# Attention plus expert layer on one core: ones laid by transfers, tables loaded ahead, multiplies before the first chunk, one chunk's remainder moved

## The reference

```
x = x + layernorm(attention(layernorm(x)))        # 16 heads, causal softmax, output projection, biases
x = x + layernorm(experts(layernorm(x)))          # top 2 of 8 experts per sequence, exact gelu, mean of both
# layernorm(x) = (x - mean) / sqrt(var + 1e-5), over the 256 features
```

## Time and profile before

| | us |
|---|---|
| median of three runs (lowest, highest) | 2064.71 (2061.21, 2065.99) |
| the profiled execution | 2067.85 |
| its span, first to last instruction | 2066.1 |
| PE, DVE, ACT, POOL busy in the span | 1978.9, 1799.9, 1362.3, 316.4 |
| mean granted TensorE clock | 0.985 |

### The profile page before, as it was taken

The page is one execution under the profiler, slowest core; times in us unless marked ns, Lnnn a source line. Parts: engine busy times, 40 slices in busy tenths (PEclk is TensorE's granted clock), DMA queues, the critical chain, the costliest instruction groups (busy, mean ns, idle before and its releaser), DMA issues.

```text
span 2066.1 us, 39584 instructions
## 1 busy us (share of the span) xinstructions
PE 1978.9 (96%) x15700; PEld 863.7 (42%) x15700; DVE 1799.9 (87%) x3564; ACT 1362.3 (66%) x1651; POOL 316.4 (15%) x366
## 2 busy tenths in 40 slices
PE   6999999999999999999999999999999996999997
PEld 3655333333333333333333333333333324666664
DVE  6876799999999999999999999999899917899873
ACT  3766657777777777777777777777777781333332
POOL 5333201010110101011100101011010104322000
PEclk9999989999999999999999999999999998999998
DMA  4877613150504224030513314050422034453220
GB/s 124 254 242 207 156 26 67 28 90 8 89 18 85 47 48 82 16 89 13 85 32 68 71 26 89 7 90 20 82 48 50 17 104 108 123 148 108 82 67 31
DMA packets 144651, 162.40 MB, mean 79 GB/s; under 512 B 52690, under 2 KB 118354, under 8 KB 144466
## 3 DMA queue, kind: packets, MB, share of 16 engines
q1 hardware_dynamic: 137554, 147.26, 30.5%
q0 software_dynamic: 6912, 12.61, 2.7%
HBM read 99.77 MB, written 59.77 MB: 77 GB/s over the span
## 4 chain that ended last, share of the span: by engine, by line
PE 79%; DVE 13%; ACT 4%; issue 1%; SPq 1%; DMA 1%; POOL 0%; ACTq 0%; DVEq 0%; POOLq 0%
PE b_psO L1103 25%; PE b_psS L1086 25%; PE b_ring L605 13%; PE a_psQK L888 6%; DVE b_pmax L621 3%; PE a_psV L900 3%; PE c_psH L1483 3%; PE c_psO L1496 2%; ACT b_prob L1050 2%; PE b_ring L603 1%; DVE c_attn L105 1%; DVE c_ln_f_stats L81 1%; DVE c_ln_x_stats L81 1%; PE c_psA L1453 1%; DVE c_x L1314 1%
## 5 line engine op out<-in xcount | busy, mean ns | idle before, releaser
L621 DVE TENSOR_REDUCE b_pmax<-b_ring 128x1 f32<-128x512 f32 (+4 forms) x2284 | 1336.6, 647 | 82.1 <-PE b_ring L605 65.1
L1050 ACT ACTIVATE b_prob<-b_psS 128x1024 f32<-128x1024 f32 (+3 forms) x1280 | 1085.1, 895 | 372.2 <-PE b_psS L1086 367.5
L1086 PE MATMUL b_psS<-g_qT,g_kT 64*128 64x512 bf16 (+6 forms) x5120 | 837.5, 349 | 10.0 <-ACT b_prob L1050 7.2
L605 PE MATMUL b_ring<-g_kT,g_qT 64*128 64x512 bf16 (+2 forms) x2500 | 717.5, 349 | 4.0 <-DVE b_pmax L621 2.6
L1103 PE MATMUL b_psO<-b_prob,g_v 128*32 128x512 f32 (+3 forms) x5120 | 597.3, 542 | 0.3
L1086 PEld LDWEIGHTS b_psS<-g_qT,g_kT 64*128 64x128 bf16 (+1 forms) x5120 | 296.6, 94 | 462.9 <-ACT b_prob L1050 343.4
L1021 POOL TENSOR_SCALAR_AFFINE_SELECT b_prob<-b_prob 128x512 f32<-128x512 f32 x256 | 164.5, 643 | 1321.1 <-ACT b_prob L1050 1320.9
L605 PEld LDWEIGHTS b_ring<-g_kT,g_qT 64*128 64x128 bf16 x2500 | 221.7, 94 | 236.3 <-DVE b_pmax L621 163.7
L603 PE MATMUL b_ring<-later,query_of 64*128 64x128 bf16 x988 | 192.4, 220 | 1.9 <-DVE b_pmax L621 1.3
L1103 PEld LDWEIGHTS b_psO<-b_prob,g_v 128*32 128x32 f32 x5120 | 103.6, 108 | 174.2 <-issue 132.8
L1483 PE MATMUL c_psH<-c_yT,c_w1e 128*128 128x512 f32 x256 | 121.0, 618 | 20.8 <-ACT c_hT L1408 20.7
(11 more groups left out here) (113 smaller groups left out, 1059.4 us busy)
## 6 DMA issues: line engine op xcount, KB each, us to landing
qk_parts<-a_parts SPq DMA_DIRECT2D x64, 384.0 KB, 4.6
g_qT<-qk_parts SPq DMA_DIRECT2D x184, 128.0 KB, 3.9
g_kT<-qk_parts SPq DMA_DIRECT2D x184, 128.0 KB, 5.2
out_sums<-b_outT SPq DMA_DIRECT2D x64, 256.0 KB, 2.6
v_ones<-a_v SPq DMA_DIRECT2D x16, 544.0 KB, 6.0
g_v<-v_ones SPq DMA_DIRECT2D x32, 272.0 KB, 5.3
a_x<-in_L_attn_x SPq DMA_DIRECT2D x16, 512.0 KB, 4.8
c_x<-in_L_attn_x SPq DMA_DIRECT2D x16, 512.0 KB, 6.9
```

Source lines behind the costliest of these rows:

```text
L605: ins_ = self.nc.tensor.matmul(to, groups.qT[own, g, h // 2, 0, t * P:(t + 1) * P], groups.kT[own, g, h // 2, 0, pc * CH:pc * CH + w], sta ...
L621: self.nc.vector.tensor_reduce(pmax[:, c % 2].rearrange("p (h t) n -> p h t n", t=TT)[:, heads[0]:heads[-1] + 1:2, qt, pc], bank[:, 0:k * ...
L1050: nc.scalar.activation(prob[:, j % PBUF, 2 * s:2 * s + 2, off:CH], psS[:, 2 * s:2 * s + 2, off:CH], ACT.Exp).then_inc(exp_done, 1)
L1086: ins_ = nc.tensor.matmul(psS[:, 2 * s + p, off:CH], kT[own, g, s, ab, kt * P:(kt + 1) * P], qT[own, g, s, ab, c * CH + off:(c + 1) * CH], ...
```

## The change

`write_ones` now fills a small tile of ones, 128 partitions of 16 elements, and clears the part of `g_v`. A new method `lay_ones` starts eight DMAs on POOL's queue, after the tables of `build_rest`; each copies the small tile into one row of 2048 elements of the key tile, and stage B's PE waits for them. ACT takes a root of a constant as its first instruction, and an exponential of it during chunk 14, both into a tile `a_ready` that nobody reads. PE multiplies the identity with itself 36 times into the value bank before it waits for the first chunk, and waits for the weights after the first transposes instead of before them. The last chunk's middle part, low part and store move from key steps 1, 3 and 6 to 26, 30 and 34.

```diff
-    SET_ONES = 3
+    SET_ONES = 2
+    LAID = 2 * 2 * HP
...
+        self.ones_laid = ctx.enter_context(nc.semaphore("g_ones_laid"))
+        self.ones = ctx.enter_context(nc.sbuf_tensor("g_ones", [P, S // P], BF16))
...
     def write_ones(self, pool):
+        self.nc.gpsimd.memset(self.ones[:, :], 1.0).then_inc(self.ones_set, 1)
+        self.nc.gpsimd.memset(self.vS[:, :, :, HG * VC:VROW].rearrange("p g t n -> p (g t) n"), 0.0
+                              ).then_inc(self.ones_set, 1)
+
+    def lay_ones(self, eng):
+        eng.wait_ge(self.ones_set, self.SET_ONES)
         for p in range(2):
             row = p * HALF + KB
-            self.nc.gpsimd.memset(self.kT[row:row + 1, :, :, 1, :], 1.0).then_inc(self.ones_set, 1)
-        pool.wait_ge(self.ones_set, 2)
-        self.nc.gpsimd.memset(self.vS[:, :, :, HG * VC:VROW].rearrange("p g t n -> p (g t) n"), 0.0
-                              ).then_inc(self.ones_set, 1)
+            for g in range(2):
+                for s in range(HP):
+                    eng.dma_start(self.kT[row:row + 1, g, s, 1, :].rearrange("o (p n) -> o p n", p=P),
+                                  self.ones[:, :]).then_inc(self.ones_laid, 16)
...
-REST_MIDDLE_AT = 1
-REST_LOW_AT = 3
-REST_STORED_AT = 6
+REST_MIDDLE_AT = 26
+REST_LOW_AT = 30
+REST_STORED_AT = 34
...
+        WARM = 36
...
+        ready = sb("a_ready", [P, 2], F32)
...
             consts.build_rest(pool)
+            groups.lay_ones(pool)
...
             act.wait_ge(consts.set, consts.EPS_SET)
+            nc.scalar.activation(ready[:, 0:1], consts.eps[:, :], ACT.Sqrt)
             root(0)
...
                 if n + 2 < N:
                     root(n + 2)
+                elif n + 2 == N:
+                    nc.scalar.activation(ready[:, 1:2], consts.eps[:, :], ACT.Exp)
...
             pe.wait_ge(consts.set, consts.IDENT)
+            for i in range(WARM):
+                nc.tensor.matmul(psV[:, i % TT, 0:P], ident[:, :], ident[:, :], start=True, stop=True)
+            turn(0)
             pe.wait_ge(w_ld, 5 * 16)
-            turn(0)
...
-            pe.wait_ge(groups.ones_set, Groups.SET_ONES)
+            pe.wait_ge(groups.ones_laid, 16 * Groups.LAID)
```

## The result

| | before | changed |
|---|---|---|
| median of 11 runs each (us) | 2065.99 | 2052.11 |
| lowest, highest | 2058.71, 2071.63 | 2046.39, 2056.98 |
| profiled execution, its span | 2067.85, 2066.1 | 2049.51, 2047.8 |

The ratio is 0.9937, 95% interval 0.992 to 0.9953: 13.9 us less by the medians, where 12.8 were forecast. The measured median is within 0.2 us of the forecast of 2052.

The account below looks back on a forecast made before the run. PE (96% busy) was taken to bound the kernel, with DVE (87%) where it is later. Start 10.0 plus stage B 5.5 minus new places 2.7 gave 12.8 us off 2064.71, so 2052 us, range 2049 to 2056 (8 in 10: 2046 to 2059).

Parts of the forecast that it names:

- Memsets and first table load: Start of stage A: without the memsets' delay of DVE (6.7 us) and the table load (1.28), first chunk 8.0 us earlier.
- PE's own multiplies are late next: Start of stage A: multiplies end at 11.9 us, then transposes and copy, first L888 at 13.8, a gain of 7.1 us.
- Full clock for chunk 0: Chunk 0's first query-key matmuls take 6.87 us instead of 9.75 if the clock is up: 2.9 us gained.
- What hides: POOL's eight issues end at 13 to 14.5 us with 10 us of cover; chunk 14's early exponential costs 0, at most 0.2.
- third rival: Laying the ones is slow, 2.5 us per issue, so POOL is free at 28 us: 2055 to 2056 us; chance 0.06.
- Stage B's first 30 us: 217.77 to 247.8 us: table load, low and middle part go; gain 5.5 us, between 3.5 and 7.5.
- none there: Near 231 us in stage B: no clock dip expected once the wait for the low part and the table load are gone.
- The new places: Stage B: low part at step 30 costs 2.2 us, middle part at step 26 0.5, stores 0; together -2.7 us.
- second rival: The dip at 286 us, 13.6 us at half clock, goes too as PE's rhythm changes: 2048 us; chance 0.17.
- A low part with a dip behind it: First rival: the low part at step 30 stops PE and the clock falls, up to 5.1 us more: 2057; chance 0.17.
- A clock that is not held: Fourth rival: the multiplies do not raise the clock, L888 starts at 19.9 us, the start gives 1.0: 2061; chance 0.10.
- Two dips in the first group: Fifth rival: the clock falls repeatedly from 218 us; two more dips eat the gain, three or more give 2071; chance 0.06.

Follow-up runs that it names:

- e1: Kernel before with only the ones laid by eight transfers instead of two memsets: chunk 1's matmuls start 6.7 us earlier; 73.5 us to step 22.
- e12: The changed kernel itself, timed again on one chip with the POOL version: median 2051.75 us, ratio 0.9934 to the kernel before.
- e3: Changed kernel without the 36 multiplies: first query-key matmul at 13.23 us, chunk 1 at 26.25 against 24.96.
- e4: Changed kernel with the last chunk's middle part, low part and store back at steps 1, 3 and 6: 73.0 us to step 22 instead of 66.1.
- e2: Kernel before with only the 36 multiplies and the moved wait for the weights: first query-key matmul at 21.03 us, chunk 1 0.4 us later.
- e6: Kernel before with the two memsets cut in four each: L888 started at 20.39 us instead of 20.94; 73.5 us to step 22.
- e7: Changed kernel with only the middle part back at step 1: 66.8 us to step 22, 115.3 to step 38.
- e10: Changed kernel with the last chunk's middle and low part on POOL and 28 multiplies instead of 36: chunk 1 at 26.40 us, ratio 0.9918 to the kernel before.
- e5: Changed kernel without the early exponential in chunk 14: 67.6 us to step 22, 1.5 us later; 120.2 to step 38.

## Why the prediction was right, step by step

- **Memsets and first table load.** 8.0 us forecast; the first chunk was ready at 9.4 us, as said, from a start of the statistics 0.2 us later. e1 shows the memsets' share, 6.7 us at chunk 1.
- **PE's own multiplies are late next.** Forecast start of L888 13.8, measured 13.70, on the path that was forecast: the chain goes through L896, then the transposes, then the copy. But three terms were off and cancelled. The clock rose 3.6 us after the first multiply and not 5.3 (the first 17 records stand in 3.6 us, 0.21 each; 5 or 6 weight loads per us up to 4.6 us, 10 or 11 from 5.3 on); by the prediction's own prices the block would have ended at 11.1, and it ended at 11.63, about half of that because a record took 0.112 us at full clock and not 0.107; and transposes, copy and hand-overs took 2.07 instead of 1.87. The moment of the rise varies from run to run: 3.0 to 5.7 us after the first multiply in the eight traces, 3.6 in the changed kernel and 4.9 in e12, which is the same kernel. What sets it is not shown.
- **Full clock for chunk 0.** 2.9 us forecast, 9.89 - 7.24 = 2.65 measured. But e3 shows that leaving the multiplies out costs only 1.3 us: the slow records there took 8.85 us, not 9.75, and L906 started 0.5 us earlier. The larger part of stage A's gain, 8.6 of 9.9 us in these two traces, needs no multiplies.
- **What hides.** POOL was free at 12.2 us (eight issues, 4.69 us), before the 13 to 14.5 forecast, and 12 us ahead of L787 at 24.61. Three of the eight issues ran beside the four L105 and took 0.64 to 0.77 us; the five behind them took 0.54 each (lines in the last section). So POOL's issues were at most 0.23 us longer beside instructions of 0.41 us, and the four L105 took 1.38. The third rival's 2.5 us for one issue did not come; the dearest of the eight took 0.77. The exponential ahead of time cost stage A nothing: 9.89 us of gain at chunk 1 and 9.88 at the last chunk.
- **Stage B's first 30 us: the term that was mis-sized.** 5.5 us forecast. Against the one trace it was 8.0, like with like 73.5 - 66.1 = 7.4. What failed is "DVE cannot be fed without a gap through a ring of three banks": it is, for 21.02 us. The floor that I had worked out, 22.5 us, was the answer, and I took the middle between two bounds instead of asking which engine was left to stop DVE. The reason given for the dip at 231 us, the wait for the low part, fits the profile of before and e4; in e1, e2 and e6 the clock fell ahead of the low part, behind the table load. The prediction removed both, so its "none there" came true.
- **The new places.** -2.7 forecast, -3.8 measured. Low: 2.2 forecast, 2.1 measured. Middle: 0.5 forecast, 1.7 measured; I read ACT's busy share (18.68 of 25) as slack, but an exponential behind the 1.89 us is what PE waits for next, and PE waited 1.8 us. At step 1 the same part costs 0.7.
- **The sum.** Stage B 5.5 - 2.7 = 2.8 forecast, 3.5 measured like with like; stage A 10.0 forecast, 8.9 to 10.2 measured in eight traces against the one profile of before. Together 12.4 to 13.7, and 13.9 by the medians. Two errors of about 1 us and 2 us in stage B had opposite signs, and so had those of the first start; that the median was met to 0.1 us is partly luck.
- **The rivals.** The dip at 286 is neither fixed nor caused by the change: it was 13.7, 6.8 or 0 us in the traces, with and without the change. So the second rival can't be told from scatter. A low part with a dip behind it came in e7. A clock that is not held came in e10. Two dips in the first group came in the changed stage B in e5 and e7, three in no trace.

Not settled: what decides the length of the second dip, and whether the clock falls behind the table load. The second dip's place is after the stretch with DVE full, in every kernel that shows it. Of the 11 timed runs of the changed kernel the three fastest (2046.4 to 2049.5 us) have a mean clock of 0.990 to 0.992 and the four slowest (2056.0 to 2057.0) one of 0.986 to 0.988, so much of the scatter goes with time at half clock. In the traces most of that time lies in stage C (35.5 us in the changed kernel's trace, against 6.8 in the first group), which I didn't study.

## What to carry to other kernels

Look at what a long instruction on few partitions keeps from running elsewhere: 13.9 us of memsets on one partition, on an idle engine, cost 6.7 us at the start, and cutting them did not help. When the first waits of a stage go, the gain is bounded by the busiest engine's own work; here that bound, DVE's 22.5 us of 30.0, was the answer. A dip of the clock seen in one trace needs more traces before a cause is named: its place and length differed between runs of the same stage. Put leftover work where an engine really is idle in the order that its neighbours wait for, not where its busy share looks low.

## What was not expected of the hardware

Eight transfers of 4 KB in pieces of 32 bytes, issued by POOL, landed in 4.8 to 5.5 us each, and the four L105 beside their issues kept their length: 1.38 us together, as in chunk 1 of the kernel before (20.23 us). The line on them in the changed kernel's view of DMA issues:

```profile
g_kT<-g_ones POOLq DMA_DIRECT2D x8, 4.0 KB, 5.1
```

The issues up to 9.4 us, beside the four L105 (lengths in ns):

```profile
L286 POOL DMA_DIRECT2D g_kT<-g_ones x3: 637/655/770, 7.5 to 8.9; - x3
```

POOL's cast of 128x2048 took 1.89 us, as long as ACT's (1.89), and its subtraction 4.08 beside a DVE at full pace. The clock fell after an idle time of PE of 3.05 us in e10, and at 231 us of the kernel before after several shorter ones. The waits of PE in that kernel from 215 to 232 us (total, times, longest):

```profile
PE b_psS L1086 <- ACT b_prob L1050: 1.6, 2, 1.1
PE b_ring L605 <- DVE b_pmax L621: 1.3, 1, 1.3
PE b_ring L605 <- ACT a_v L831: 0.9, 1, 0.9
```

In the changed kernel only the last of the three is left before 235 us, and the clock stays up. Waits of 0.9 and 1.1 us alone came before a fall in e2 and before none in e5, so the sum of the waits does not decide it in these traces.
